# Row maxima taken one row-tile pair earlier, and a third PSUM buffer in the three feed-forward stages

## The chip, the cores and the metric

The kernel runs on all 8 cores of one Trainium2 chip, with no exchange between the cores. The metric is the time on the device in microseconds (us) of the slowest core; the figure shown for a kernel is the median of its runs.

## The reference, cut to what matters

The input x is 4 sequences of 4096 tokens with 1024 features, in float32. One layer is computed, attention first and then a gated feed-forward part, each behind a layer norm without weights:

```python
q = x @ Wq; k = x @ Wk; v = x @ Wv          # x is the normed input, 64 features out
att = softmax(einsum('bid,bkd->bik', q, k), axis=1)   # over i, the query axis
x = x + tile(att @ v, 16)
xr = mu_r*z + (1-mu_r)*z_prev;  xk = mu_k*z + (1-mu_k)*z_prev   # z = layernorm(x)
r = sigmoid(xr @ W_r.T);  k_act = relu(xk @ W_k.T)**2
x = x + r * (k_act @ W_v.T)
```

The softmax runs over the query axis, so a row-tile of 128 keys needs one maximum and one sum for each of its keys over all 4096 queries, and the sum is folded into the rows of v.

## The kernel before, in words

Two cores share a sequence. Each norms all 4096 tokens and computes attention for them, and then does the feed-forward part for its own 2048. The program is written engine by engine; its stages follow one another through counting semaphores (SM for TensorE, SV for VectorE, SS for ScalarE). The order on each engine is the order in which its instructions are written, and the counts waited for are computed by small functions (`d_max`, `d_ellsum`, `d_exp`, `d_outmm`, `i_sig`, `j_relu`, `k_tmp`), so a reordering of VectorE's work needs a new count for each of its instructions.

**Attention (lines 519 to 590, here stage D).** There are 32 row-tiles kt of 128 keys, worked in 16 groups q of two (a = 0 and 1, kt = 2q + a). A group has eight units: s = 0 to 3 (a stretch of 1024 queries), and in each of them a = 0, then a = 1. A unit is two score matmuls (L548, 64 rows, 512 columns each) into one of three PSUM units, then one exponential on ScalarE (L608) with the negated maximum as bias, which also leaves a partial sum in `ellp`. Below, the units of a group are u0 to u7. In program order:

- TensorE, group q: it first does the eight "out" matmuls (L529) of group q-2, which wait for the scaled v of that group, and then the 16 score matmuls of u0 to u7. A unit's scores wait for the exponential three units earlier, which frees its PSUM unit. Out matmuls and the next group's u0 therefore stand behind u7's scores of the group before.
- ScalarE, group q: eight exponentials. Before u0 and u1 (s = 0) it waits, in this order, for the row-tile's maximum (`d_max(kt)`), for the sum of the row-tile two earlier (`d_ellsum(kt-2)`, since that one's partial sums lie in the same columns of `ellp`), for out matmuls that free the buffer `p_sb` (`d_outmm(kt-4)`), and for the unit's scores (`d_smm`).
- VectorE, group q (lines 568 to 590): two maxima (L573, over every fourth column of the first 512 of u0 and of u1), then for each of the two row-tiles, once its eighth part's exponential is done, the sum (L579), its reciprocal (L583), the scaling of v (L586) and a small copy (L589).

In VectorE's order of before, the maxima of group q+1 stand behind all eight small instructions of group q.

**Feed-forward.** Stage H (L866 to L888) forms xr and xk: ScalarE scales, VectorE adds. Stage I (L899 to L923): 16 tiles of 16 matmuls (L909) into two PSUM buffers `rps` of 1024 columns, each evacuated by a sigmoid (L922); ScalarE waits for the end of stage H before its first sigmoid, while TensorE starts as soon as xr is complete. Stage J (L940 to L977): 32 tiles of 8 matmuls (L949) into two buffers `ktp` of 512 columns, relu on ScalarE (L965), square on VectorE (L974). Stage K (L997 to L1063): 16 tiles of 16 matmuls (L1006) into two buffers `ops` of 1024 columns; VectorE multiplies by r (L1051), adds attention's output (L1055) and x (L1061), and SyncE's queue writes y (L1029). In all three, TensorE waits for the reader of the tile two earlier before it reuses a buffer (L906, L947, L1003).

Of the kernel before, what the change touches and what calls it, by code (L numbers as in the profile page):

```python
# [7 lines left out]
F32 = mybir.dt.float32  # L8
BF16 = mybir.dt.bfloat16
AF = mybir.ActivationFunctionType  # L10
# [4 lines left out]
C = 1024  # L15
# [4 lines left out]
KT = 32  # L20
# [6 lines left out]
def build_program(debug=False):  # L27
    nc = bass.Bass("TRN2", target_bir_lowering=False)
# [32 lines left out]
    with ctx:  # L61
# [32 lines left out]
        def opens(cms):  # L94
            return [cm.__enter__() for cm in cms]
# [38 lines left out]
        SV = e(nc.semaphore("SV"))  # L134
        SS = e(nc.semaphore("SS"))
# [70 lines left out]
        SM_D0, SS_D0, SV_D0 = SM_C, SS_A, SV_C  # L206
# [12 lines left out]
                return SM_D0 + d_P(q + 2) - 4 * (1 - (t % 2))  # L219
            return SM_D0 + 368 + 8 * (q - 14) + 4 * (t % 2 + 1)  # L220
        d_exp = lambda kt, s: SS_D0 + 8 * (kt // 2) + 2 * s + (kt % 2) + 1
        d_max = lambda kt: SV_D0 + 10 * (kt // 2) + (kt % 2) + 1
        d_ellsum = lambda kt: SV_D0 + 10 * (kt // 2) + 3 + 4 * (kt % 2)
        d_recip = lambda kt: SV_D0 + 10 * (kt // 2) + 4 + 4 * (kt % 2)
        d_vsc = lambda kt: SV_D0 + 10 * (kt // 2) + 5 + 4 * (kt % 2)
        d_xp = lambda kt: SV_D0 + 10 * (kt // 2) + 6 + 4 * (kt % 2)
        SM_D = SM_D0 + 384
        SS_D = SS_D0 + 128
        SV_D = SV_D0 + 160
        e_evac = SV_D + 2  # L230
        e_tpmm = lambda b: SM_D + b + 1
        e_oxmm = SM_D + 16 + KT
# [58 lines left out]
        i_sig = lambda t: SS_I0 + t + 1  # L291
# [4 lines left out]
        j_relu = lambda ix: SS_J0 + ix + 1  # L296
# [6 lines left out]
        k_tmp = lambda t: SV_K0 + 3 * t + 1  # L303
# [261 lines left out]

        @block.vector
        def _(v):
            for q in range(KT // 2):
                for a in range(2):
                    kt = 2 * q + a  # L570
                    u0 = d_eidx(kt, 0) % 3
                    v.wait_ge(SM, d_smm(kt, 1))
                    v.reduce_max(negm[:, kt:kt + 1],  # L573
                                 units[u0][:, 0:512:4],
                                 axis=AX.X, negate=True).then_inc(SV, 1)
                for a in range(2):
                    kt = 2 * q + a
                    v.wait_ge(SS, d_exp(kt, 3))
                    v.reduce_sum(ell[:, kt:kt + 1],  # L579
                                 ellp[:, 4 * (kt % 2):4 * (kt % 2) + 4],  # L580
                                 axis=AX.X).then_inc(SV, 1)
                    v.wait_ge(SV, d_ellsum(kt))
                    v.reciprocal(rell[:, kt:kt + 1], ell[:, kt:kt + 1]).then_inc(SV, 1)  # L583
                    v.wait_ge(SV, d_recip(kt))
                    v.wait_ge(SVT, 16 * (kt + 2))
                    v.tensor_scalar(vs_sb[:, kt * D:(kt + 1) * D],  # L586
                                    v_sb[:, kt * D:(kt + 1) * D],
                                    rell[:, kt:kt + 1], None, ALU.mult).then_inc(SV, 1)
                    v.tensor_copy(xp_sb[:, kt:kt + 1],  # L589
                                  p_sb[kt % 4][:, 4095:4096]).then_inc(SV, 1)  # L590

        @block.scalar
        def _(sc):
# [299 lines left out]
        closes(z1T_cm)  # L893
        r_sb_cm = [nc.sbuf_tensor("r_sb", [128, TOWN * C], BF16, side="right")]
        r_sb, = opens(r_sb_cm)
        cm_rps = [nc.psum_tensor(f"rps{i}", [128, C], F32) for i in range(2)]
        r_ps = opens(cm_rps)

        @block.tensor  # L899
        def _(t):  # L900
            t.wait_ge(SV, h_xr_all)
            t.wait_ge(SS, SS_F)
            t.wait_ge(SWB, SWB_ALL)
            for t_ in range(TOWN):
                if t_ >= 2:
                    t.wait_ge(SS, i_sig(t_ - 2))  # L906
                for ct in range(CT):
                    for hh in range(2):
                        ins = t.matmul(  # L909
                            r_ps[t_ % 2][:, hh * 512:(hh + 1) * 512],  # L910
                            xr[ct][:, t_ * 128:(t_ + 1) * 128],
                            wrT[:, ct * C + hh * 512:ct * C + (hh + 1) * 512],
                            start=(ct == 0), stop=(ct == CT - 1),
                            skip_group_check=True)
                ins.then_inc(SM, 1)

        @block.scalar
        def _(sc):
            sc.wait_ge(SV, SV_H)
            for t_ in range(TOWN):  # L920
                sc.wait_ge(SM, i_mm(t_))
                sc.activation(r_sb[:, t_ * C:(t_ + 1) * C], r_ps[t_ % 2][:, :],  # L922
                              AF.Sigmoid).then_inc(SS, 1)  # L923

        closes(cm_rps)
# [8 lines left out]

        kaT_cm = [nc.sbuf_tensor(f"kaT{i}", [128, 2048], BF16, side="right") for i in range(CT)]
        kaT = opens(kaT_cm)
        cm_ktp = [nc.psum_tensor(f"ktp{i}", [128, 512], F32) for i in range(2)]
        kt_ps = opens(cm_ktp)

        @block.tensor  # L940
        def _(t):
            t.wait_ge(SS, SS_I)
            for dt in range(CT):
                for tc in range(4):
                    ix = dt * 4 + tc
                    if ix >= 2:
                        t.wait_ge(SS, j_relu(ix - 2))  # L947
                    for ct in range(CT):
                        ins = t.matmul(  # L949
                            kt_ps[ix % 2][:, :],  # L950
                            wkT[:, ct * C + dt * 128:ct * C + (dt + 1) * 128],
                            xk[ct][:, tc * 512:(tc + 1) * 512],
                            start=(ct == 0), stop=(ct == CT - 1),
                            skip_group_check=True)
                    ins.then_inc(SM, 1)

        @block.scalar
        def _(sc):
            for dt in range(CT):
                for tc in range(4):  # L960
                    ix = dt * 4 + tc
                    sc.wait_ge(SM, j_mm(ix))
                    if ix >= 4:
                        sc.wait_ge(SV, j_sq(ix - 4))
                    sc.activation(kaT[dt][:, tc * 512:(tc + 1) * 512],  # L965
                                  kt_ps[ix % 2][:, :], AF.Relu).then_inc(SS, 1)

        @block.vector
        def _(v):
# [21 lines left out]
        k32_cm = [nc.sbuf_tensor("tmp32", [128, 2 * C], F32, side="right"),  # L991
                  nc.sbuf_tensor("x2b", [128, 2 * C], F32, side="right")]
        tmp32, x2b = opens(k32_cm)
        cm_ops = [nc.psum_tensor(f"ops{i}", [128, C], F32) for i in range(2)]
        o_ps = opens(cm_ops)

        @block.tensor  # L997
        def _(t):
            t.wait_ge(SV, SV_J)
            t.wait_ge(SS, SS_J)  # L1000
            for t_ in range(TOWN):
                if t_ >= 2:
                    t.wait_ge(SV, k_tmp(t_ - 2))  # L1003
                for dt in range(CT):
                    for hh in range(2):
                        ins = t.matmul(  # L1006
                            o_ps[t_ % 2][:, hh * 512:(hh + 1) * 512],
                            kaT[dt][:, t_ * 128:(t_ + 1) * 128],
                            wvT[:, dt * C + hh * 512:dt * C + (hh + 1) * 512],
                            start=(dt == 0), stop=(dt == CT - 1),  # L1010
                            skip_group_check=True)
                ins.then_inc(SM, 1)
# [29 lines left out]
        @block.vector  # L1042
        def _(v):
            for t_ in range(TOWN):
                s = t_ % 4
                v.wait_ge(SM, k_mm(t_))
                v.wait_ge(SS, i_sig(t_))
                if t_ >= 2:
                    v.wait_ge(SV, k_x2(t_ - 2))
                    v.wait_ge(YSs[t_ % 2], ys_k(t_ - 2))  # L1050
                v.tensor_tensor(tmp32[:, (t_ % 2) * C:(t_ % 2 + 1) * C],  # L1051
                                o_ps[t_ % 2][:, :],
                                r_sb[:, t_ * C:(t_ + 1) * C], ALU.mult).then_inc(SV, 1)
                v.wait_ge(SV, k_tmp(t_))
                v.tensor_tensor(tmp32[:, (t_ % 2) * C:(t_ % 2 + 1) * C],  # L1055
                                tmp32[:, (t_ % 2) * C:(t_ % 2 + 1) * C],
                                bass.AP(out_tok, t_ * D, [[TOWN * D, 128], [0, 16], [1, D]]),
                                ALU.add).then_inc(SV, 1)
                v.wait_ge(FSs[t_ % 8], fs_k(t_))
                v.wait_ge(SV, k_mid(t_))  # L1060
                v.tensor_tensor(x2b[:, (t_ % 2) * C:(t_ % 2 + 1) * C],  # L1061
                                tmp32[:, (t_ % 2) * C:(t_ % 2 + 1) * C],
                                xst[:, (t_ % 8) * C:(t_ % 8 + 1) * C], ALU.add).then_inc(SV, 1)  # L1063
# [59 lines left out]
```

## Time and profile before

| what | value |
|---|---|
| median of 2 runs | 727.45 us (727.39 to 727.5) |
| the profiled execution | 728.75 us |
| its span, slowest core (core 3) | 727.1 us |
| spans of the eight cores | 717.6 to 727.1 us |
| mean granted TensorE clock of the cores | 0.706 to 0.729 of full speed |
| busy share: TensorE matmul, VectorE, ScalarE | 50%, 41%, 38% |

The span reaches from the first to the last instruction of one core; the run's time has 1.65 us more (728.75 less 727.1), which lie around it. A row of the profile gives a start, a duration, the engine, the line of the program, the output and input names, and in brackets how long the engine sat idle before and what released it. The granted clock is 1 at 2.4 GHz and 0.5 at 1.2 GHz. Times of single instructions on core 3 are given from the start of its span.

### The profile page before, as it was taken

The numbers are of one execution on the slowest core, as the hardware profiler recorded it, in microseconds if no ns is written. First come the engines' busy times: TensorE is split into PE (matmuls) and PEld (weight loads), VectorE is DVE, ScalarE is ACT, GpSimd is POOL, SyncE is SP. The second block draws the span as 40 slices with busy tenths as digits, with TensorE's granted clock in tenths as the row PEclk, the third lists the DMA queues.
The fourth block names the chain that finished last, engine by engine and source line by source line (L and its number), as shares of the span: only waits on it lengthen the run. The fifth ranks groups of instructions, "written<-read, shape, count | busy, mean of one in ns | idle before, by whom it ended". The sixth has DMA issues, their size and how long they took to land.

```text
span 727.1 us, 5705 instructions; the slowest of 8 cores (717.6 to 727.1 us)
## 1 busy us (share of the span) xinstructions
PE 362.9 (50%) x1392; PEld 124.3 (17%) x1392; DVE 296.7 (41%) x515; ACT 276.4 (38%) x437; POOL 25.4 (3%) x45
## 2 busy tenths in 40 slices
PE   0004000007967888888862000000439999999873
PEld 0001000003411111111112000000114434444331
DVE  3904508057711111111121598806860002228886
ACT  3205022050038898889860233206842233320000
POOL 2000000000000030000000011000000000011110
PEclk9999555557985555555565555555569999999997
DMA  9965977827010099900000044293100000007774
GB/s 235 284 160 132 276 115 250 191 80 173 1 32 7 6 138 160 288 7 0 1 0 1 5 165 181 71 178 73 29 0 1 0 1 1 0 21 269 255 227 154
DMA packets 79044, 75.82 MB, mean 104 GB/s; under 512 B 59427, under 2 KB 59443, under 8 KB 78948
## 3 DMA queue, kind: packets, MB, share of 16 engines
q1 hardware_dynamic: 25700, 41.01, 17.6%
q0 software_dynamic: 10944, 23.93, 14.2%
q10 hardware_dynamic: 42368, 10.52, 8.8%
q8 instruction: 12, 0.20, 0.1%
q14 instruction: 20, 0.16, 0.1%
HBM read 47.79 MB, written 21.56 MB: 95 GB/s over the span
## 4 chain that ended last, share of the span: by engine, by line
DMA 31%; PE 22%; DVE 20%; issue 12%; ACTq 7%; ACT 6%; SPq 2%; DVEq 1%
DMA v_sb<-vdram 14%; PE ktp L949 7%; PE rps L909 7%; ACTq L366 5%; DMA zdram<-zst 4%; DMA z1T<-z1dram 4%; DMA y_out<-x2b 4%; ACT p_sb L608 3%; DVE x1b L739 3%; DVE xk L888 3%; DVE sums L419 2%; DVE zst L407 2%; ACTq L831 2%; DMA xst<-x_in 2%; DVE tmp L1055 2%
## 5 line engine op out<-in xcount | busy, mean ns | idle before, releaser
L608 ACT ACTIVATE p_sb<-dpool,negm 128x1024 bf16<-128x1024 f32 x128 | 140.6, 1124 | 21.9 <-DVE negm L573 21.9
L909 PE MATMUL rps<-wrT,xr 128*128 128x512 bf16 x256 | 60.4, 402 | 142.0 <-DVE xr L881 130.0
L548 PE MATMUL dpool<-qrep,krep 64*128 64x512 bf16 x256 | 109.9, 601 | 33.6 <-ACT p_sb L608 28.3
L447 PE MATMUL qk<-zT,wqk 128*128 128x512 bf16 x64 | 18.1, 434 | 160.1 <-DVE qrep L478 98.5
L352 ACT ACTIVATE zst<-xst 128x1024 bf16<-128x1024 f32 x32 | 33.8, 1057 | 97.6 <-issue 86.0
L1006 PE MATMUL ops<-wvT,kaT 128*128 128x512 bf16 x256 | 57.2, 379 | 11.3 <-DVE tmp L1051 9.7
L579 DVE TENSOR_REDUCE ell<-ellp 128x1 f32<-128x4 f32 x32 | 5.0, 157 | 134.7 <-ACT p_sb L608 134.7
L949 PE MATMUL ktp<-xk,wkT 128*128 128x512 bf16 x256 | 55.6, 379 | 1.7 <-ACT r_sb L922 1.3
L909 PEld LDWEIGHTS rps<-wrT,xr 128*128 128x128 bf16 x256 | 26.2, 103 | 175.9 <-issue 148.9
L974 DVE TENSOR_TENSOR kaT<-kaT 128x512 bf16<-128x512 bf16 x32 | 13.6, 425 | 98.1 <-ACT kaT L965 98.0
L419 DVE TENSOR_REDUCE sums<-xst 128x1 f32<-128x1024 f32 x32 | 37.1, 1211 | 10.9 <-DMA xst<-x_in 10.9
L548 PEld LDWEIGHTS dpool<-qrep,krep 64*128 64x128 bf16 x256 | 16.7, 104 | 125.0 <-issue 124.8
L447 PEld LDWEIGHTS qk<-zT,wqk 128*128 128x128 bf16 x64 | 6.7, 107 | 169.5 <-issue 163.9
L376 DVE TENSOR_SCALAR smean<-sums,cconst 128x4 f32<-128x4 f32 x12 | 2.8, 229 | 78.4 <-ACT zst L352 76.9
L965 ACT ACTIVATE kaT<-ktp 128x512 bf16<-128x512 f32 x32 | 19.0, 597 | 34.5 <-PE ktp L949 34.5
L1006 PEld LDWEIGHTS ops<-wvT,kaT 128*128 128x128 bf16 x256 | 24.2, 97 | 44.3 <-issue 16.8
L816 ACT ACTIVATE zst<-x1b 128x1024 bf16<-128x1024 f32 x16 | 16.9, 1057 | 36.1 <-DVE x1b L739 36.1
L949 PEld LDWEIGHTS ktp<-xk,wkT 128*128 128x128 bf16 x256 | 24.9, 98 | 32.3 <-issue 2.6
L922 ACT ACTIVATE r_sb<-rps 128x1024 bf16<-128x1024 f32 x16 | 16.3, 1024 | 36.6 <-PE rps L909 36.6
L881 DVE SCALAR_TENSOR_TENSOR xr<-z1T,mu1m,xr 128x2048 bf16<-128x2048 bf16 x8 | 18.8, 2351 | 26.8 <-ACT xr L866 26.7
L608 ACT ACTIVATION_READ_ACCUMULATOR p_sb<-dpool,negm 128x1 f32 x128 | 27.7, 216 | 0.0
L529 PE MATMUL dpool<-p_sb,v_sb 128*64 128x512 bf16 x112 | 26.9, 634 | 0.0
(83 smaller groups left out, 371.8 us busy)
## 6 DMA issues: line engine op xcount, KB each, us to landing
xst<-x_in SPq DMA_DIRECT2D x32, 512.0 KB, 9.0
xst<-x_in POOLq DMA_DIRECT2D x32, 512.0 KB, 7.2
zdram<-zst SPq DMA_DIRECT2D x32, 256.0 KB, 7.7
y_out<-x2b SPq DMA_DIRECT2D x16, 512.0 KB, 4.2
z1dram<-z1b SPq DMA_DIRECT2D x16, 256.0 KB, 3.2
wrT<-wrT_in POOLq DMA_DIRECT2D x1, 2048.0 KB, 18.8
wkT<-wkT_in POOLq DMA_DIRECT2D x1, 2048.0 KB, 30.7
wvT<-wvT_in POOLq DMA_DIRECT2D x1, 2048.0 KB, 44.0
```

The source lines that it names most:

```text
L352: sc.activation(zst[:, (i % 8) * C:(i % 8 + 1) * C], xst[:, (i % 8) * C:(i % 8 + 1) * C], AF.Square, accum_out=sumsq[:, i % 8:i % 8 + 1]). ...
L366: sc.dma_start(out=zT[ctn][:, qtr * 1024:(qtr + 1) * 1024], in_=zdram[qtr * 1024:(qtr + 1) * 1024, ctn * 128:(ctn + 1) * 128], transpose=T ...
L419: v.reduce_sum(sums[:, i % 8:i % 8 + 1], xst[:, (i % 8) * C:(i % 8 + 1) * C], axis=AX.X).then_inc(SV, 1)
L447: t.matmul(qk[buf][:, :], wqk[:, ct * 128:(ct + 1) * 128], zT[ct][:, nch * 512:(nch + 1) * 512], start=(ct == 0), stop=(ct == CT - 1), ski ...
L529: t.matmul(dpool[64 * half:64 * half + 64, (w % 2) * 512:(w % 2) * 512 + 512], vs_sb[:, tt_ * D:(tt_ + 1) * D], p_sb[tt_ % 4][:, w * 512:( ...
L548: t.matmul(units[u][:, cc * 512:(cc + 1) * 512], krep[64 * a:64 * (a + 1), kt * 128:(kt + 1) * 128], qrep[64 * a:64 * (a + 1), c * 512:(c ...
L608: sc.activation(p_sb[kt % 4][:, s * 1024:(s + 1) * 1024], units[u][:, :], AF.Exp, bias=negm[:, kt:kt + 1], accum_out=ellp[:, 4 * (kt % 2) + s:
L739: v.tensor_tensor(x1b[:, s8 * C:(s8 + 1) * C], xst[:, s8 * C:(s8 + 1) * C], bass.AP(out_tok, t_ * D, [[TOWN * D, 128], [0, 16], [1, D]]), ...
L888: v.scalar_tensor_tensor(xk[ct][:, :], z1T[ct][:, 15:2063], mu1m[:, 8 + ct:9 + ct], xk[ct][:, :], ALU.mult, ALU.add).then_inc(SV, 1)
L909: ins = t.matmul(r_ps[t_ % 2][:, hh * 512:(hh + 1) * 512], xr[ct][:, t_ * 128:(t_ + 1) * 128], wrT[:, ct * C + hh * 512:ct * C + (hh + 1) ...
L949: ins = t.matmul(kt_ps[ix % 2][:, :], wkT[:, ct * C + dt * 128:ct * C + (dt + 1) * 128], xk[ct][:, tc * 512:(tc + 1) * 512], start=(ct == ...
L1006: ins = t.matmul(o_ps[t_ % 2][:, hh * 512:(hh + 1) * 512], kaT[dt][:, t_ * 128:(t_ + 1) * 128], wvT[:, dt * C + hh * 512:dt * C + (hh + 1) ...
```

## The change

It does two things. In attention, VectorE takes the maxima of groups 0 and 1 first, and then, behind the eight small instructions of group q, the maxima of group q+2 instead of q+1; the counts are recomputed by a table. In stages I, J and K the PSUM buffers are three instead of two, and TensorE waits for the reader of the tile three earlier.

```diff
+        D_CNT = {}
+        _sv = SV_D0
+        for _kt in range(4):
+            _sv += 1
+            D_CNT[("max", _kt)] = _sv
+        for _q in range(16):
+            for _a in range(2):
+                _kt = 2 * _q + _a
+                for _op in ("ellsum", "recip", "vsc", "xp"):
+                    _sv += 1
+                    D_CNT[(_op, _kt)] = _sv
+            if _q + 2 < 16:
+                for _a in range(2):
+                    _sv += 1
+                    D_CNT[("max", 2 * (_q + 2) + _a)] = _sv
+        d_max = lambda kt: D_CNT[("max", kt)]
...
         @block.vector
         def _(v):
-            for q in range(KT // 2):
+            def d_maxes(v, q):
                 for a in range(2):
                     kt = 2 * q + a
                     u0 = d_eidx(kt, 0) % 3
...
                     v.reduce_max(negm[:, kt:kt + 1],
                                  units[u0][:, 0:512:4],
                                  axis=AX.X, negate=True).then_inc(SV, 1)
+
+            d_maxes(v, 0)
+            d_maxes(v, 1)
+            for q in range(KT // 2):
                 for a in range(2):
                     kt = 2 * q + a
                     v.wait_ge(SS, d_exp(kt, 3))
...
+                if q + 2 < KT // 2:
+                    d_maxes(v, q + 2)
...
-        cm_rps = [nc.psum_tensor(f"rps{i}", [128, C], F32) for i in range(2)]
+        cm_rps = [nc.psum_tensor(f"rps{i}", [128, C], F32) for i in range(3)]
...
-                if t_ >= 2:
-                    t.wait_ge(SS, i_sig(t_ - 2))
+                if t_ >= 3:
+                    t.wait_ge(SS, i_sig(t_ - 3))
...
-        cm_ktp = [nc.psum_tensor(f"ktp{i}", [128, 512], F32) for i in range(2)]
+        cm_ktp = [nc.psum_tensor(f"ktp{i}", [128, 512], F32) for i in range(3)]
...
-                    if ix >= 2:
-                        t.wait_ge(SS, j_relu(ix - 2))
+                    if ix >= 3:
+                        t.wait_ge(SS, j_relu(ix - 3))
...
-        cm_ops = [nc.psum_tensor(f"ops{i}", [128, C], F32) for i in range(2)]
+        cm_ops = [nc.psum_tensor(f"ops{i}", [128, C], F32) for i in range(3)]
...
-                if t_ >= 2:
-                    t.wait_ge(SV, k_tmp(t_ - 2))
+                if t_ >= 3:
+                    t.wait_ge(SV, k_tmp(t_ - 3))
```

The indices of the buffers change from `% 2` to `% 3` with it, in the matmuls and in their readers.

## Rows read from the trace of the kernel before

**Rows 1.** Page, costliest groups: the exponentials, with the idle time before them.

```profile
L608 ACT ACTIVATE p_sb<-dpool,negm 128x1024 bf16<-128x1024 f32 x128 | 140.6, 1124 | 21.9 <-DVE negm L573 21.9
```

**Rows 2.** Timeline of TensorE alone, core 3: one group's out matmuls in attention.

```profile
260.77 1.92 PE L529 MATMUL dpool<-p_sb,v_sb 128*64 128x512 bf16 x8
```

**Rows 3.** The same, matmuls that run between 262.9 and 263.2 us.

```profile
262.62 1.04 PE L548 MATMUL dpool<-qrep,krep 64*128 64x512 bf16 x4
```

**Rows 4.** Timeline of all engines, core 3, the same group change.

```profile
254.10 1.11 ACT L608 ACTIVATE p_sb<-dpool,negm 128x1024 bf16<-128x1024 f32 x1 [1.47 <-DVE negm L573]
...
259.47 0.22 ACT L608 ACTIVATION_READ_ACCUMULATOR p_sb<-dpool,negm 128x1 f32 x1
...
259.80 0.14 PEld L548 LDWEIGHTS dpool<-qrep,krep 64*128 64x128 bf16 x2 [0.96 <-issue]
...
261.99 0.16 DVE L579 TENSOR_REDUCE ell<-ellp 128x1 f32<-128x4 f32 x1 [7.95 <-ACT p_sb L608]
262.25 0.16 DVE L583 RECIPROCAL rell<-ell 128x1 f32<-128x1 f32 x1
...
262.74 0.24 ACT L608 ACTIVATION_READ_ACCUMULATOR p_sb<-dpool,negm 128x1 f32 x1
...
263.08 0.16 DVE L579 TENSOR_REDUCE ell<-ellp 128x1 f32<-128x4 f32 x1 [0.20 <-ACT p_sb L608]
...
263.84 0.15 DVE L589 COPY xp_sb<-p_sb 128x1 bf16<-128x1 bf16 x1
263.90 0.48 DVE L573 TENSOR_REDUCE negm<-dpool 128x1 f32<-128x128 f32 x2
264.44 1.11 ACT L608 ACTIVATE p_sb<-dpool,negm 128x1024 bf16<-128x1024 f32 x1 [1.47 <-DVE negm L573]
```

**Rows 5.** Line 573's durations in ns (least, median, most), core 3.

```profile
L573 DVE TENSOR_REDUCE negm<-dpool x32: 277/280/292, 207.8 to 367.5; 128x1 f32<-128x128 f32 x32
```

**Rows 6.** Timelines of single engines, core 3, start of attention and its first group change.

```profile
207.13 0.61 PE L548 MATMUL dpool<-qrep,krep 64*128 64x512 bf16 x4 [0.94 <-DVE p_sb L482]
...
207.82 0.49 DVE L573 TENSOR_REDUCE negm<-dpool 128x1 f32<-128x128 f32 x2 [0.84 <-PE dpool L548]
...
222.59 0.48 DVE L573 TENSOR_REDUCE negm<-dpool 128x1 f32<-128x128 f32 x2
...
220.33 0.23 ACT L608 ACTIVATION_READ_ACCUMULATOR p_sb<-dpool,negm 128x1 f32 x1
...
223.07 1.11 ACT L608 ACTIVATE p_sb<-dpool,negm 128x1024 bf16<-128x1024 f32 x1 [1.41 <-DVE negm L573]
```

**Rows 7.** Stretches: TensorE busy (matmuls), clock, DMA share, GB/s; core 0, then core 3.

```profile
214.00:368.00 154.00, 118.36 (x354) 0.63 0.37 72
...
214.00:368.00 154.00, 129.73 (x352) 0.50 0.37 72
```

**Rows 8.** Timeline, core 3, start of the sigmoid stage.

```profile
519.50 9.83 PE L909 MATMUL rps<-wrT,xr 128*128 128x512 bf16 x32 [130.00 <-DVE xr L881]
...
541.38 18.86 PE L909 MATMUL rps<-wrT,xr 128*128 128x512 bf16 x77 [12.04 <-ACT r_sb L922]
545.60 14.36 PEld L909 LDWEIGHTS rps<-wrT,xr 128*128 128x128 bf16 x67 [0.28 <-issue]
```

**Rows 9.** Timeline, core 3, start of the relu stage.

```profile
593.23 3.61 PE L949 MATMUL ktp<-xk,wkT 128*128 128x512 bf16 x16 [1.26 <-ACT r_sb L922]
...
597.23 2.97 PE L949 MATMUL ktp<-xk,wkT 128*128 128x512 bf16 x13 [0.39 <-ACT kaT L965]
```

**Rows 10.** Line 1051, core 3: what it waited for, then who waited for it.

```profile
  DMA y_out<-x2b: 7.9, 6
  PE ops L1006: 4.0, 1
...
  PE ops L1006: 9.7, 11
```

More of the change, by code:

```diff
@@ L221, in build_program @@
         d_exp = lambda kt, s: SS_D0 + 8 * (kt // 2) + 2 * s + (kt % 2) + 1
[L222 to L226, printed above, removed]
+        D_CNT = {}
[14 more added lines that the diff above has]
+        d_max = lambda kt: D_CNT[("max", kt)]
+        d_ellsum = lambda kt: D_CNT[("ellsum", kt)]
+        d_recip = lambda kt: D_CNT[("recip", kt)]
+        d_vsc = lambda kt: D_CNT[("vsc", kt)]
+        d_xp = lambda kt: D_CNT[("xp", kt)]
         SM_D = SM_D0 + 384
         SS_D = SS_D0 + 128
-        SV_D = SV_D0 + 160
+        SV_D = _sv
+        assert SV_D == SV_D0 + 160
         e_evac = SV_D + 2
@@ L909, in _ @@
                         ins = t.matmul(
-                            r_ps[t_ % 2][:, hh * 512:(hh + 1) * 512],
+                            r_ps[t_ % 3][:, hh * 512:(hh + 1) * 512],
                             xr[ct][:, t_ * 128:(t_ + 1) * 128],
@@ L921, in _ @@
                 sc.wait_ge(SM, i_mm(t_))
-                sc.activation(r_sb[:, t_ * C:(t_ + 1) * C], r_ps[t_ % 2][:, :],
+                sc.activation(r_sb[:, t_ * C:(t_ + 1) * C], r_ps[t_ % 3][:, :],
                               AF.Sigmoid).then_inc(SS, 1)
@@ L945, in _ @@
                     ix = dt * 4 + tc
-                    if ix >= 2:
-                        t.wait_ge(SS, j_relu(ix - 2))
+                    if ix >= 3:
+                        t.wait_ge(SS, j_relu(ix - 3))
                     for ct in range(CT):
                         ins = t.matmul(
-                            kt_ps[ix % 2][:, :],
+                            kt_ps[ix % 3][:, :],
                             wkT[:, ct * C + dt * 128:ct * C + (dt + 1) * 128],
@@ L965, in _ @@
                     sc.activation(kaT[dt][:, tc * 512:(tc + 1) * 512],
-                                  kt_ps[ix % 2][:, :], AF.Relu).then_inc(SS, 1)
+                                  kt_ps[ix % 3][:, :], AF.Relu).then_inc(SS, 1)
         @block.vector
@@ L1006, in _ @@
                         ins = t.matmul(
-                            o_ps[t_ % 2][:, hh * 512:(hh + 1) * 512],
+                            o_ps[t_ % 3][:, hh * 512:(hh + 1) * 512],
                             kaT[dt][:, t_ * 128:(t_ + 1) * 128],
@@ L1051, in _ @@
                 v.tensor_tensor(tmp32[:, (t_ % 2) * C:(t_ % 2 + 1) * C],
-                                o_ps[t_ % 2][:, :],
+                                o_ps[t_ % 3][:, :],
                                 r_sb[:, t_ * C:(t_ + 1) * C], ALU.mult).then_inc(SV, 1)
```

## The prediction

> **What bounds the kernel now.** I read the page's costliest groups first. The exponentials of attention are its largest item, 140.6 us, with 21.9 us of idle time before them, all put down to the maxima [rows 1]: 15 group changes at 1.46 us. This is what the new order of VectorE addresses. The question is what holds the exponential once the maximum no longer stands behind eight other instructions, so next I took the timelines around one group change, TensorE alone [rows 2, 3] and all engines [rows 4].
>
> ScalarE's period is 10.34 us (254.10 to 264.44): eight exponentials at 1.09, and a wait of 1.47. The last exponential's accumulator read ends at 262.98, yet u0 of the next group starts at 264.44 [rows 4]. VectorE is busy with its small instructions until 263.99 and starts the maxima at 263.90. TensorE, though, is hardly earlier. u7's scores could only be written once u4's exponential had ended at 259.69; they start by 259.83, the eight out matmuls follow at 260.77, and the next group's u0 scores not before 262.62 [rows 2 to 4]. Four score matmuls, those of u0 and u1, overlap and end at 262.62 + 1.04 = 263.66 [rows 3]. So two chains, through VectorE and through TensorE, end within 0.24 us of each other (263.66 and 263.90), and only the first is shortened.
>
> For the feed-forward stages I read the gaps of TensorE. Stage I starts with two tiles at 519.50, ends them at 529.33, and then waits 12.04 us for the first sigmoid, which ScalarE cannot start before stage H is done [rows 8]. After that TensorE runs without a gap. Stage J has a gap of 0.39 us before its third tile [rows 9]. In stage K TensorE waits 9.7 us for VectorE, while VectorE waits only once for TensorE, at the start (4.0 us), and 7.9 us for writes of y [rows 10].
>
> **Attention, steady group changes (14 of the 15).** The maxima's release moves from VectorE's own queue to TensorE's semaphore. At the start of the stage four matmuls end at 207.13 + 0.61 = 207.74, and the maximum that they release starts at 207.82 [rows 6]: 0.08 us. So maximum 0 starts at 263.66 + 0.08 = 263.74 instead of 263.90. Two maxima take 0.48 and one of them 0.28, so the second starts 0.20 behind the first [rows 4, 5], at 263.94, and ends at 264.22.
>
> That would give back 0.16, but there is a second edge. ScalarE's u0 also waits for the sum of the row-tile two earlier, L579. Before, that sum was done at 262.15, long ahead. In the new order it is queued behind both maxima of the next group, which wait for TensorE. It starts when they have passed: an instruction without a dependency starts about 0.09 before the end of the one ahead (copy to 263.99, maximum at 263.90) [rows 4], so at 264.13, and ends 0.16 later at 264.29. Then ScalarE: before, maximum 0 ended at 264.18 and the exponential began at 264.44, 0.26 later, with three more waits in its queue. At the first group change, where there are two more, it is 222.59 + 0.28 to 223.07, 0.20 [rows 5, 6]. I read 0.06 for each further wait. Behind the sum two are left, so 0.20: the exponential starts at 264.49, 0.05 later than before. Times 14, +0.7 us.
>
> Its bounds: if the sum did not count, 263.74 + 0.28 + 0.26 = 264.28, a gain of 0.16 each or 2.2 us in all. If u1's matmuls came a slot of 0.43 later than I read (4 matmuls in 1.04 us against 604 to 635 ns for one leaves little room), nothing on VectorE overlapped, and each step paid the 0.10 between a sum and its reciprocal (262.15 to 262.25), the start would be 263.66 + 0.43 + 0.08 + 0.28 + 0.10 + 0.16 + 0.20 = 264.91, a loss of 0.47 each or 6.6 us. I stay with +0.05, since the pairing is seen in rows 3. Behind the waiting maxima stand also reciprocal, scaling and copy of both row-tiles. The scaled v is needed by out matmuls a whole group later, and the second sum must be there for u1, 1.09 us behind u0. From a sum to the start of what follows its copy is 0.82 (263.08 to 263.90) [rows 4], so the second sum runs from 264.95 to 265.11 and would let u1 go at 265.31, against 264.49 + 1.09 = 265.58: hidden, with 0.27 of cover. If that cover were gone, u1 would take over as the one that waits.
>
> **The first group change** has no out matmuls in TensorE's queue. There u6's exponential ends at 220.56 [rows 6], u1's scores start 0.25 later and take a slot and a matmul (0.43 + 0.61), to 221.85; maximum at 221.93 to 222.21, sum to 222.28, exponential with one further wait (0.14) at 222.42 instead of 223.07: -0.65, between 0 and -1.4 (the whole wait). Attention together: +0.7 - 0.65, about +0.1 us, from -3.6 to +6.6.
>
> **Stage I.** With a third buffer, tile 2 is computed inside the 12.04 us wait. It costs 16 slots; in the fast stretch 67 weight loads take 14.36 us, 0.215 each [rows 8], so 3.45 us. It fits, leaving 8.6 idle, and 13 tiles instead of 14 stand behind the first sigmoid: -3.45 us. The clock: the first stretch after the wait runs at half speed, from 541.38 to 545.60, about 10 slots of 0.43. I keep that cost, since 8.6 us of idle are left. If it vanished, another 10 x 0.21 = 2.1 us would go; if it were as much longer, 2.1 come back.
>
> **Stage J.** The 0.39 us before the third tile [rows 9] go, as its buffer is free: -0.39, between 0 and that. Nothing else waits there. **Stage K.** TensorE's 9.7 us of waits are off the chain: VectorE has three instructions of 1.23 to a tile, and waits for writes of y. TensorE runs one tile further ahead, and nobody starts sooner. 0 us.
>
> The Trainium skill (Perfetto Trace Analysis, Optimization Strategy) says that a gap that keeps repeating on the engine that should be saturated can mean that too few buffers fit in SBUF or PSUM. Stage K's waits on TensorE have that look, and by that rule the third buffer would give them back; here the rows of VectorE say that TensorE is not that engine. It is a rival below.
>
> **Sum.** 728.75 + 0.1 - 3.45 - 0.39 = 725.0 us for the profiled execution. That one ran 1.30 above the median of 727.45, so 723.7 us for the median.
>
> **Rivals.**
> - *The wait of ScalarE closes.* For it: all 21.9 us are put down to the maxima [rows 1]. Against it: TensorE's u0 at 262.62. Then the time is 723.7 - 0.1 - 21.9 = 701.7. TensorE at full clock would do most of it: u7's, the out and u0's matmuls take eight slots or so at half speed. With slots of 0.21, u1's scores would follow u6's exponential (ended 261.88) as at the first group change but quicker, at 262.7, and the exponential could start at 263.25, -1.19 each, 17 us in all, so about 706. On core 3 the clock stood at 0.50 over the 154 us; on core 0 it was 0.63 on average [rows 7], and since a core's place in the order by time can change, some chance stays. Chance of either 0.06. The Trainium skill (TensorE: Matmul & The Clock Gate, on why this matters for kernels) holds that TensorE kept busy without gaps gets the full clock; core 3, busy for 9 of 10.3 us, shows that this doesn't come by itself.
> - *Stage K gives back TensorE's 9.7 us.* For it: 11 waits for L1051; against it: VectorE's only wait for TensorE is the first tile's. 723.7 - 9.7 = 714.0. Chance 0.05.
> - *The sum behind the maxima costs more (slower).* One place: L579 behind L573 in VectorE's queue, with ScalarE's u0 behind it. At its upper bound attention loses 6.6 - 0.65, and the total is 728.75 + 5.95 - 3.84 = 730.9, or 729.6 against the median. The change turns slower than before once a group change costs over 0.32 us more (14 x 0.32 = 4.5, as much as the other terms give). For it: three serial steps behind a late TensorE; against: the overlaps seen in rows 3 and 4. Chance 0.12.
> - *The new order gains nothing and the rest neither* (the idle stretch in stage I costs more cold slots, or writes of y in stage K eat what comes early, as their 7.9 us depend on what else moves): 726 to 729. Chance 0.10.
>
> **How the numbers follow.** My forecast, 723.7 with its own 719.5 to 726, has 0.67. The range of 8 in 10 is 719.5 to 728.5: it has the forecast's low end (attention -2.2 and the cold stretch gone -2.1, near 719.5) and most of the last two rivals; about 0.11 lies below, in the two fast rivals, and under 0.09 above. A measurement of this kernel tells about 2%, 14.5 us, from no change. Faster by over that, under 712.9, is only the first rival: 0.06. Slower by over that, above 742, has no case that I can price: 0.02. Within 2%: 0.92.
>
> **What would show it.** In the changed profile: the wait before u0's exponential still about 1.5 us at 14 of 15 group changes, now put down to the sum L579 (or TensorE) rather than L573; the maxima starting 0.08 us behind TensorE's matmuls and ahead of L579; a first group change about 0.8 us wide; stage I starting with 48 matmuls in a row and about 8.6 us of idle behind them; no wait of 0.39 in stage J; in stage K fewer waits of TensorE and the same length from first L1051 to the end. A group change under 1 us wide would overturn the reading of TensorE's chain; a shorter stage K, that of VectorE's.

## The result, and the profile after

The changed kernel runs in 723.8 us (median of 21 runs, 721.1 to 730.7) against 730.1 us for the kernel before in the same rounds (median of 20, 726.3 to 733.5). The ratio is 0.9923, with a 95% interval of 0.9902 to 0.9944: a gain of 0.8%. The forecast was 723.7 against 727.45, a ratio of 0.9948, with the range 719.5 to 728.5. The kernel before has medians of 727 to 734 us in the different sets of runs, so ratios are used from here on; they leave out the few executions in which the cores ran longer at a lower granted clock.

The profiled execution took 725.28 us, with a span of 723.7 on its slowest core, now core 1. Its costliest groups, next to [rows 1]:

```profile
L630 ACT ACTIVATE p_sb<-dpool,negm 128x1024 bf16<-128x1024 f32 x128 | 140.5, 1124 | 22.3 <-PE dpool L564 17.0
L931 PE MATMUL rps<-wrT,xr 128*128 128x512 bf16 x256 | 59.6, 398 | 141.7 <-DVE xr L903 132.6
...
L589 DVE TENSOR_REDUCE negm<-dpool 128x1 f32<-128x128 f32 x32 | 7.9, 287 | 129.9 <-PE dpool L564 129.9
L1028 PE MATMUL ops<-wvT,kaT 128*128 128x512 bf16 x256 | 56.5, 379 | 6.7 <-DVE tmp L1073 5.2
```

The exponentials' idle time is 22.3 us where it was 21.9, and has changed its name: most of it is now put down to TensorE's scores instead of the maxima, and the maxima themselves wait for TensorE, 129.9 us in all. The program's lines have moved: 573 is now 589, 608 is 630, 548 is 564.

A group change of attention, timeline of all engines on core 1 (start, duration, engine, line, what; in brackets the idle time before), next to [rows 3, 4]:

```profile
257.47 1.92 PE L545 MATMUL dpool<-p_sb,v_sb 128*64 128x512 bf16 x8
...
259.32 1.89 PE L564 MATMUL dpool<-qrep,krep 64*128 64x512 bf16 x6
259.43 0.24 ACT L630 ACTIVATION_READ_ACCUMULATOR p_sb<-dpool,negm 128x1 f32 x1
...
260.46 0.49 DVE L589 TENSOR_REDUCE negm<-dpool 128x1 f32<-128x128 f32 x2 [7.99 <-PE dpool L564]
260.87 0.15 DVE L599 TENSOR_REDUCE ell<-ellp 128x1 f32<-128x4 f32 x1
261.12 0.16 DVE L603 RECIPROCAL rell<-ell 128x1 f32<-128x1 f32 x1
261.22 1.11 ACT L630 ACTIVATE p_sb<-dpool,negm 128x1024 bf16<-128x1024 f32 x1 [1.55 <-PE dpool L564]
...
271.64 1.11 ACT L630 ACTIVATE p_sb<-dpool,negm 128x1024 bf16<-128x1024 f32 x1 [1.55 <-PE dpool L564]
```

The order is the one that the prediction drew: eight out matmuls, u0's and u1's scores at 259.32, both maxima at 260.46, the sum behind them at 260.87, and the exponential at 261.22. The period is 10.42 us (261.22 to 271.64) where it was 10.34. The profile names TensorE as the releaser; the sum ended at 261.02, later than anything of TensorE's that this exponential needs, so the name alone would mislead.

The start of the sigmoid stage and of the relu stage, timeline of core 1, next to [rows 8, 9]:

```profile
519.98 12.88 PE L931 MATMUL rps<-wrT,xr 128*128 128x512 bf16 x48 [132.65 <-DVE xr L903]
...
541.85 3.55 PE L931 MATMUL rps<-wrT,xr 128*128 128x512 bf16 x8 [9.00 <-ACT r_sb L944]
...
589.84 12.46 PE L971 MATMUL ktp<-xk,wkT 128*128 128x512 bf16 x57 [1.26 <-ACT r_sb L944]
```

48 matmuls now run before the wait instead of 32, the wait is 9.00 instead of 12.04 us, and in stage J the matmuls run on past the second tile. Line 1073 (L1051 before), what it waited for and then who waited for it, next to [rows 10]:

```profile
  DMA y_out<-x2b: 8.5, 5
  PE ops L1028: 4.0, 1
...
  PE ops L1028: 5.2, 7
```

TensorE waits less in stage K: 5.2 us on this core, where the same core had 6.7 before and core 3 had 9.7. VectorE waits as before. By stage, from the first and last start of the stages' lines on each core, the means of the eight cores:

| stage (us) | before | after | forecast for the difference |
|---|---|---|---|
| attention, first to last exponential | 162.65 | 162.4 | +0.1 |
| I, first matmul to stage J's first | 73.5 | 70.4 | -3.45 |
| J, to stage K's first matmul | 57.5 | 57.0 | -0.39 |
| K, first matmul to the last L1061 (L1083) | 70.6 | 70.7 | 0 |

The mean of attention hides two kinds of cores: 162.8 to 163.1 us on six, 161.0 and 160.6 on cores 3 and 4. The start of attention and the stretch from its end to stage I differ by some us from core to core and from run to run in both kernels.

### The profile page after: what moved, and what is told of

Same layout as the page of the kernel before. It is cut to its first block, busy times and chain, and to the rows that moved or that the text cites. A ratio compares the mean times of both kernels' runs of the same rounds, so it can differ in the third digit from the quotient of the medians.

```text
span 723.7 us, 5702 instructions; the slowest of 8 cores (712.3 to 723.7 us)
## 1 busy us (share of the span) xinstructions
PE 356.0 (49%) x1392; PEld 124.5 (17%) x1392; DVE 295.6 (41%) x515; ACT 276.2 (38%) x437; POOL 25.4 (4%) x45
## 4 chain that ended last, share of the span: by engine, by line
DMA 30%; PE 28%; DVE 19%; issue 9%; ACTq 7%; ACT 5%; SPq 2%; DVEq 1%
DMA v_sb<-vdram 13%; PE ktp L971 8%; PE rps L931 6%; ACTq L382 5%; DMA zdram<-zst 4%; DMA z1T<-z1dram 4%; PE dpool L564 4%; DMA xst<-x_in 3%; DMA y_out<-x2b 3%; PE ops L1028 3%; DVE x1b L761 3%; DVE xk L910 3%; ACT p_sb L630 2%; DVE sums L435 2%; ACTq L853 2%
## 5 line engine op out<-in xcount | busy, mean ns | idle before, releaser
L630 ACT ACTIVATE p_sb<-dpool,negm 128x1024 bf16<-128x1024 f32 x128 | 140.5, 1124 | 22.3 <-PE dpool L564 17.0
L564 PE MATMUL dpool<-qrep,krep 64*128 64x512 bf16 x256 | 104.0, 575 | 39.8 <-DVE xp_sb L609 19.8
L589 DVE TENSOR_REDUCE negm<-dpool 128x1 f32<-128x128 f32 x32 | 7.9, 287 | 129.9 <-PE dpool L564 129.9
```

What stands on the lines that cost most here:

```text
L564: t.matmul(units[u][:, cc * 512:(cc + 1) * 512], krep[64 * a:64 * (a + 1), kt * 128:(kt + 1) * 128], qrep[64 * a:64 * (a + 1), c * 512:(c ...
L630: sc.activation(p_sb[kt % 4][:, s * 1024:(s + 1) * 1024], units[u][:, :], AF.Exp, bias=negm[:, kt:kt + 1], accum_out=ellp[:, 4 * (kt % 2) + s:
```

## The experiments

Nine runs follow: eight kernels, one of them twice. Each is set against the kernel before as it ran in the same rounds.

### e1_order: VectorE's order alone

```diff
 (the change, with the buffers of stages I, J and K back at two)
-        cm_rps = [nc.psum_tensor(f"rps{i}", [128, C], F32) for i in range(3)]
+        cm_rps = [nc.psum_tensor(f"rps{i}", [128, C], F32) for i in range(2)]
...
```

> Only VectorE's new order; stages I, J, K keep two buffers. Theory (TensorE's chain through u7's scores, the eight out matmuls and u0's scores sets the exponential of u0 as much as VectorE did, and the sum L579 is now queued behind the waiting maxima): attention keeps its length, a group change costs 10.42 us instead of 10.34 (10.24 on a core whose clock rises inside u0's scores), the first change 0.67 instead of 1.41. Time within 1 us of before, ratio 0.997 to 1.002. Rival (the order of VectorE was what held ScalarE, and the gain of the change is its): 3 to 6 us faster, ratio 0.992 to 0.996.

Measured: 729.25 against 728.56 us, ratio 1.0005 (0.997 to 1.004). Attention: 162.8 and 162.9 us on cores 2 and 5, 160.6 to 161.1 on the other six. The first and last exponential of core 5, what it waited for, and then the same of core 0:

```profile
L630 ACT ACTIVATE p_sb<-dpool,negm x128: 1106/1122/1152, 212.4 to 375.3; 128x1024 bf16<-128x1024 f32 x128
...
  PE dpool L564: 17.0, 11
  DVE ell L599: 5.0, 4
```

```profile
L630 ACT ACTIVATE p_sb<-dpool,negm x128: 1103/1120/1147, 207.5 to 368.1; 128x1024 bf16<-128x1024 f32 x128
...
  DVE ell L599: 19.8, 15
```

The wait of 22 us is there on core 5, and 19.8 us of it on core 0: the new order removed the cause that was named [rows 1], and the wait stayed. The 2 us that six cores save in attention don't show in the time (ratio 1.0005). The rival, that the gain of the change is the order's, falls.

### e2_buffers: the third buffers alone

```diff
 (the kernel before, with)
-        cm_rps = [nc.psum_tensor(f"rps{i}", [128, C], F32) for i in range(2)]
+        cm_rps = [nc.psum_tensor(f"rps{i}", [128, C], F32) for i in range(3)]
...
 (ktp and ops and the three waits likewise)
```

> Only the third buffers in stages I, J and K; VectorE's old order. Theory: stage I shorter by 3.2 us, J by 0.5, K unchanged, so -3.7 us, ratio 0.995, nearly all that the change brings. Rival (order of VectorE brings it): under 1 us. Rival (stage K gives back its waits too): K shorter by several us and the ratio under 0.985.

Measured: 726.26 against 728.56 us, ratio 0.9948 (0.9915 to 0.998). Stage I is 70.2 to 71.0 us on the eight cores, J 56.9 to 57.0, attention 162.6 to 162.9. This is the change's gain, within the intervals. The product of the two parts' ratios, 1.0005 x 0.9948 = 0.9953, lies just above the change's interval (0.9902 to 0.9944), and well within what the parts' own intervals allow.

### e7_k_only: the third buffer in stage K alone

```diff
 (the kernel before, with)
-        cm_ops = [nc.psum_tensor(f"ops{i}", [128, C], F32) for i in range(2)]
+        cm_ops = [nc.psum_tensor(f"ops{i}", [128, C], F32) for i in range(3)]
...
-                if t_ >= 2:
-                    t.wait_ge(SV, k_tmp(t_ - 2))
+                if t_ >= 3:
+                    t.wait_ge(SV, k_tmp(t_ - 3))
```

> The third buffer in stage K alone. Theory: stage K keeps its length of 70.6 us on average over the cores, since VectorE waits for writes of y and not for TensorE, ratio 0.997 to 1.003. Rival (the 9.7 us in which TensorE waited come back): ratio near 0.987, stage K near 61 us.

Measured: ratio 0.9994 (0.9961 to 1.0028). Stage K takes 66.9 to 71.9 us on the eight cores, 69.8 on average; in e1, with two buffers, it takes 69.1. L1051 on core 7, waits and waiters:

```profile
  DMA y_out<-x2b: 6.8, 3
  PE ops L1006: 4.0, 1
...
  PE ops L1006: 4.2, 3
```

TensorE's waits fell to 4.2 us on this core, where it had 7.4 before (means of the eight cores: 3.6 and 7.3), and nothing came of it. The rule of the Trainium skill that the prediction named (Perfetto Trace Analysis, Optimization Strategy) speaks of the engine that should be saturated; here that is VectorE, with three instructions of 1.23 us to a tile, and its waits are for writes of y.

### e3_sums: the sum's edge taken away

```diff
 (the change, with)
-                                 ellp[:, 4 * (kt % 2):4 * (kt % 2) + 4],
+                                 ellp[:, 4 * (kt % 4):4 * (kt % 4) + 4],
...
-                            if kt >= 2:
-                                sc.wait_ge(SV, d_ellsum(kt - 2))
+                            if kt >= 4:
+                                sc.wait_ge(SV, d_xp(kt - 4))
...
 (accum_out of the exponential likewise into column 4 * (kt % 4) + s)
```

> The change, and each of four row-tiles in flight gets its own four columns of partial sums, so that ScalarE's u0 waits for the copy of the row-tile four earlier and no longer for the sum that is queued behind the maxima. Theory: u0's exponential starts 1.68 us behind u0's scores instead of 1.90, a group change of 10.2 us; about 3 us less than the change if the sum is the last edge. Rival (TensorE alone sets it and the sum was hidden): no difference, group change 10.42.

Measured: ratio 0.9895 (0.9858 to 0.9932), where the change alone has 0.9923. Attention takes 159.1 to 159.6 us on the eight cores. Its exponentials at two successive group changes, timeline of ScalarE, core 0:

```profile
309.91 1.11 ACT L630 ACTIVATE p_sb<-dpool,negm 128x1024 bf16<-128x1024 f32 x1 [1.34 <-DVE ell L599]
320.12 1.11 ACT L630 ACTIVATE p_sb<-dpool,negm 128x1024 bf16<-128x1024 f32 x1 [1.34 <-DVE ell L599]
```

The wait is 1.34 instead of 1.55, the period 10.21 instead of 10.42: beside the cores of the change at 10.42, the sum cost 0.21 us at each change, as its place in the chain said (0.22). Within the chain it is the same: from u0's scores (308.21) to the exponential are 1.70 us instead of 1.90. With the first group change, whose 0.67 us of wait are gone, that makes 14 x 0.21 + 0.67 = 3.6 us, which is 163.0 less 159.4. Beside the cores at 10.24 (see below) it is 0.03 a change. The rest of the wait is TensorE's, as e4 shows. (The releaser printed is the sum again, for which this kernel doesn't wait there: it ended last before the exponential began.)

### e4_spread_sums: TensorE's queue cleared as well

```diff
 (e3, with)
-                if q >= 2:
-                    for tt_ in (2 * (q - 2), 2 * (q - 2) + 1):
-                        (wait, and the four out matmuls of tt_)
...
                             t.matmul(units[u][:, cc * 512:(cc + 1) * 512],
...
+                        if q >= 1 and 2 * s + a == 3:
+                            d_outs(2 * (q - 1))
+                        if q >= 1 and 2 * s + a == 5:
+                            d_outs(2 * (q - 1) + 1)
...
 (d_smm and d_outmm from a table of TensorE's new order; the last two row-tiles' out matmuls at the end)
```

> As e3, and TensorE does the out matmuls of group q-1 inside group q, four behind u3's scores and four behind u5's, instead of all eight ahead of group q+1. Theory (TensorE's queue ahead of u0's scores holds the exponential): ScalarE's wait at a group change falls from 1.5 us to 0.1 or less, 15 times, so some 19 to 21 us off attention and a time near 704. Rival (TensorE at half clock has no room for the out matmuls anywhere, since 8 units of 0.86 and 4 slots of 0.43 make 8.6 us of 8.74): waits appear inside the group instead and the gain is under half, 6 to 10 us. Rival (the wait at a group change is VectorE's): none.

Measured: 704.11 against 728.56 us, ratio 0.9648 (0.9595 to 0.9701). Attention takes 141.1 to 141.4 us on the eight cores. The exponentials on core 0: first and last start, and who waited for whom.

```profile
L644 ACT ACTIVATE p_sb<-dpool,negm x128: 1104/1120/1169, 212.9 to 354.0; 128x1024 bf16<-128x1024 f32 x128
...
  DMA vdram<-p_sb: 49.0, 1
```

The only wait left in front of an exponential is the one at the start of the stage. 162.65 less 141.3 are 21.4 us, nearly the 21.9 us of [rows 1], and it took three edits: the maxima's place on VectorE, the out matmuls on TensorE, and the sum for which ScalarE waits. The 127 steps from the first exponential to the last would be 138.4 us at 1.09 each; the other 2.9 us lie inside the groups, where one step in each is 1.27 (269.40 to 270.67 on core 0), the one to u4, whose scores stand behind four out matmuls.

### e5_spread_old and e6_spread: each without one of the others

```diff
 (e5: the kernel before with third buffers and e4's order of TensorE; VectorE's order and ellp as before)
 (e6: the change with e4's order of TensorE; ellp as before)
```

> Third buffers, VectorE's old order (the maxima of a group behind all small instructions of the group before), and TensorE's out matmuls spread as in e4. Theory (two chains end close together, each alone holds the exponential): freeing TensorE alone gives nothing, attention stays at 162.6 to 162.8 us from first to last exponential, time as e2_buffers, ratio about 0.995. Rival (TensorE's queue was the only bound and VectorE's order plays no part): attention near 141 us and about 704 to 706.

Measured: ratio 0.9964 (0.9929 to 1.0); attention 165.0 to 165.3 us. On core 5:

```profile
L622 ACT ACTIVATE p_sb<-dpool,negm x128: 1103/1113/1142, 216.9 to 381.9; 128x1024 bf16<-128x1024 f32 x128
...
  DVE negm L587: 21.9, 15
```

The 21.9 us stand unchanged, under the maxima's name. That attention grew by 2.4 us was not expected: the period is 10.48 instead of 10.34 (timeline: exponentials of u0 at 279.81 and 290.29), with the wait at the group change as before, so 0.14 us went inside the group, where e4 has its loss too: u4's exponential follows u3's after 1.24 us (283.09 to 284.33) instead of 1.09.

> The change with TensorE's out matmuls spread as in e4, but the partial sums shared as before, so that u0 waits for the sum L579 behind both maxima. Theory (the sum's edge costs what it did at the first group change of the changed kernel, where TensorE had no out matmuls: 0.67 us idle, some 0.8 us of period): attention near 141.3 + 15 x 0.8 = 153 us, time near 716. Rival (the sum costs only its 0.22 us, as in steady state of the change): attention near 145, time near 708. Rival (no cost): as e4.

Measured: 720.9 against 733.55 us, ratio 0.9837 (0.9792 to 0.9882); attention 151.0 to 151.5 us. Two of its group changes (timeline of ScalarE, core 6):

```profile
286.02 1.11 ACT L644 ACTIVATE p_sb<-dpool,negm 128x1024 bf16<-128x1024 f32 x1 [0.31 <-DVE ell L613]
295.76 1.11 ACT L644 ACTIVATE p_sb<-dpool,negm 128x1024 bf16<-128x1024 f32 x1 [0.73 <-PE dpool L575]
```

With TensorE out of the way, the shared columns of partial sums cost 151.4 - 141.3 = 10.1 us, three times what they cost behind TensorE (0.21 x 14 = 3). Both waits are the sum's, whatever the name: in front of the exponential of 295.76 it ended at 295.56, 0.20 us earlier. So under TensorE's chain lay a third one, through the sum, and cutting the first two alone gives back only half.

### e9_pairs, and e4 again

```diff
 (e4, with the out matmuls of group q-1 two at a time, w = 0 and 2 and then 1 and 3)
-        behind the scores of u3 (four) and u5 (four)
+        behind the scores of u2, u3 (row-tile 0) and u5, u6 (row-tile 1), two each
```

> As e4, but the out matmuls of group q-1 come in pairs (two halves of the array, one slot of 0.43 us) behind u2's, u3's, u5's and u6's scores of group q, instead of four behind u3's and four behind u5's. Theory (in e4 four out matmuls at a time hold up u4's scores, so u4's exponential comes 1.27 us behind u3's instead of 1.09, 15 times 0.18): attention shorter by some 2.5 us than e4's 141.3, near 139, and the time 2 us below e4 in the same call. Rival (the slots are only pushed to another unit, as 8.6 us of TensorE in 8.74 leave no room): attention 141 or longer.

> The kernel of e4 once more, on this chip, to set e9 against and to see whether its gain over before holds: ratio 0.96 to 0.97, attention 141.3 us.

Measured: e4 again 699.85 against 727.13 us, ratio 0.9617 (0.9573 to 0.9661), attention 141.1 to 141.3. e9 703.08, ratio 0.9674 (0.9622 to 0.9726), attention 145.8 to 145.9: 4.5 us longer, where 2.5 shorter was expected. This is a miss. Timeline of TensorE alone in e9, core 7:

```profile
269.60 1.04 PE L575 MATMUL dpool<-qrep,krep 64*128 64x512 bf16 x4
270.57 0.64 PE L554 MATMUL dpool<-p_sb,v_sb 128*64 128x512 bf16 x2
271.14 1.03 PE L575 MATMUL dpool<-qrep,krep 64*128 64x512 bf16 x2
272.11 0.64 PE L554 MATMUL dpool<-p_sb,v_sb 128*64 128x512 bf16 x2
272.68 3.70 PE L575 MATMUL dpool<-qrep,krep 64*128 64x512 bf16 x8
276.68 0.64 PE L554 MATMUL dpool<-p_sb,v_sb 128*64 128x512 bf16 x2 [0.31 <-DVE ell L613]
...
278.78 1.04 PE L575 MATMUL dpool<-qrep,krep 64*128 64x512 bf16 x4
```

The starts are what to look at. A pair of out matmuls, one slot of 0.43 us (the time from one pair's start to the next at half clock), holds the next scores back by 0.57 (270.57 to 271.14), and two score matmuls of one unit hold the outs back by 0.97 (271.14 to 272.11) for 0.86. So a change between the two kinds costs 0.11 to 0.14 us each time. e4 changes four times in a group, e9 eight times, which is 4 x 0.12, half a microsecond more.

That is not all that e9 changed. Its first pair of out matmuls stands one unit earlier than e4's, behind u2's scores, and TensorE sits idle 0.31 us in front of it in each group, 15 times and 5.0 us in all; in e4 again (core 4) TensorE never waits in front of an out matmul. The pair needs the scaled v, which VectorE has ready only at 276.43 (timeline of all engines, same core):

```profile
276.19 0.24 DVE L620 TENSOR_SCALAR v_sb<-v_sb,rell 128x64 bf16<-128x64 bf16 x1 [0.17 <-DVE rell L617]
```

The period is 9.18 us (269.60 to 278.78), of which TensorE is busy 8.87; in e4 it is 8.90 (270.67 to 279.57 on core 0). As an estimate from these rows, 9.18 - 0.31 and 9.18 - 0.48 are both below 8.90: without the wait e9 would not be longer than e4, and without the added changes it would not be either, so both seem to have a part in the 4.5 us. No run separates them. In 230 to 340 us (columns: length of the stretch, then busy time and count of TensorE, its weight loads, VectorE, ScalarE and GpSimd; granted clock; DMA):

```profile
230.00:340.00 110.00, 103.80 (x288) 17.64 (x288) 19.53 (x118) 106.09 (x193) 6.88 (x11) 0.50 0.51 100
```

TensorE has little room left there, and ScalarE now waits for it in every group. In e4 again (core 4) ScalarE is busy for 109.64 of the same 110 us, and TensorE for 95.39 at a mean clock of 0.60:

```profile
230.00:340.00 110.00, 95.39 (x297) 17.40 (x296) 20.99 (x129) 109.64 (x199) 6.89 (x11) 0.60 0.51 100
```

The version to keep is e4: 3.5 and 3.8% faster than the kernel before in its two runs.

## Why the prediction was right

**The reading of two chains held.** The prediction said that through TensorE u0's exponential could not come earlier than through VectorE. e1 shows it (ratio 1.0005), and with e4, e5 and e6 every step is there, in us of attention: VectorE freed alone gives nothing on the cores at 10.42 and 2 on those at 10.24 (e1), TensorE freed alone nothing (e5, 2.4 longer), both 11 (e6), and both with the sum 21 (e4).

**The steady group change: +0.05 forecast, +0.08 measured** on the cores whose clock stands at half in this chain. Step by step from u0's scores: maximum 1.14 us behind (forecast 1.12), sum 0.41 behind the maximum (0.39), exponential 0.35 behind the sum (0.36). The release of VectorE by TensorE took 0.10 and not 0.08. Nothing else in the chain was off by more than 0.02. u1 followed at 1.11, so the second sum was hidden, as said. Two readings in the prediction are loose, and nothing rests on them: eight exponentials at 1.09 and a wait of 1.47 make 10.19 and not 10.34, since the last exponential and its accumulator read take 1.25; and core 3's TensorE was busy for 8.7 and not 9 of 10.3 us (129.73 of 154 us) [rows 7].

**The first group change** was 0.67 us of idle instead of 1.41, -0.74, for -0.65.

**What the prediction did not have** is a second period. On cores 3 and 4 of the profiled run it is 10.24 and not 10.42, which is 2 us less in attention, and in e1 six cores of eight are like that. TensorE's granted clock rises there while u0's and u1's scores are running. Stretches on core 4, then on core 1, during these scores: TensorE busy (matmuls), granted clock, DMA:

```profile
307.00:307.25 0.25, 0.25 (x4) 0.67 0.19 45
307.25:307.50 0.25, 0.25 (x3) 1.00 0.06 1
...
260.00:260.25 0.25, 0.25 (x3) 0.50 0.76 131
260.25:260.50 0.25, 0.25 (x3) 0.50 1.04 197
```

It is not the rise as such that counts. Core 1 has one in each group as well from 292.50 on, but there it comes when u0's exponential has just begun (292.48), behind the chain, and the period stays 10.42. The prediction took the clock as 0.50 all through the chain; for the kernel before that made no difference, since VectorE stood in front: attention is 162.6 to 162.7 us on all its cores, with mean clocks from 0.50 to 0.64 in 230 to 340 us. The shorter period lies within the bound that was given for a group change (a gain of at most 0.16), and below the value taken.

**Stage I: -3.45 forecast, -3.1 measured.** A tile at full clock was computed in the wait, as said; the idle that was left is 9.00 us for 8.6. The missing 0.35 is in the clock term, which the prediction kept unchanged. Added up from the granted clock in the 12 us behind the wait, TensorE ran at half speed for 3.4 to 5.0 us on the eight cores before (mean 4.0) and for 3.4 to 5.6 after (mean 4.7). Half of the 0.65 us more is lost, 0.33. e1 and e2 agree: 4.5 and 4.9 us at half speed, stages of 73.8 and 70.5 us, and 3.25 + 0.2 is again 3.45. Why the stretch is longer was not shown. **Stage J: -0.39 forecast, -0.5 measured. Stage K: 0 and 0**, and e7 confirms it alone.

**The size of the whole** came out a little larger than forecast, 0.9923 against 0.9948, with the interval's upper end at 0.9944. That the median itself, 723.8, met the forecast of 723.7 is luck: the kernel before ran 2.7 us longer in these rounds than in the two runs that the forecast started from. The stage table accounts for 3.75 us of some 5.6. The shorter period on some cores can add up to 2 us where the slowest core has it; that it does so was not shown, and e1, where six cores have it, gained nothing. The rest may be the spread of the stages ahead of attention.

Of the rivals, the wait of ScalarE did not close with this change. Its price, 701.7 us or a ratio of 0.9646, is what e4 then reached with the other two edges cut (0.9648 and 0.9617). The other way to that price, TensorE at full clock, did not come: in 230 to 340 us the mean granted clock lay between 0.50 and 0.67 on every core of every profile, and in e9, where TensorE was busy for 103.80 of 110 us, it was 0.50 on all eight. The Trainium skill (TensorE: Matmul & The Clock Gate, on why this matters for kernels) would have TensorE at full clock when kept busy without gaps; e9 still has its gap of 0.31 us in each group, so no run here tests that.

## What to carry to other kernels

An idle time with one releaser in the profile is a wait for the last of what may be several chains. Before one is shortened, the end of each of the others is to be put beside it in one period of the timeline: here 263.66 stood against 263.90, and of the 21.9 us the maxima's new place gave back nothing alone, 0.13 us per change with the sum's wait gone as well (10.34 to 10.21, e3), and all but a little once TensorE's chain was cut too (e4). When an instruction that waits is moved forward on an in-order engine, whatever stands behind it is delayed to its release; here that was a sum for which the same consumer waited. A third buffer pays where the producer has an idle stretch to fill (stage I, 3 us), and nothing where the consumer is the bound (stage K).

## What the runs showed of the hardware that was not expected

- Changing between two kinds of matmuls on different parts of the array (64 rows by 128 columns, and 128 rows by 64 columns) cost 0.11 to 0.14 us of TensorE each time at half clock (e9, from the starts between 270.57 and 272.11). What part this has in e9's 4.5 us is open.
- The granted clock rose once per group on some cores and hardly at all on others running the same program (mean 0.67 on core 3, 0.54 on core 5 of the changed kernel, in 230 to 340 us). The period of the loop stayed at 10.24 us where the rise fell into u0's and u1's scores (cores 3 and 4), and was 10.42 us where it came behind them or not at all (cores 1 and 5).
- ScalarE started an exponential later after its last release the more satisfied waits still stood in its queue: 0.15 us with one (first group change of the changed kernel), 0.20 with two (both kernels), 0.26 with three (the kernel before). I read some 0.06 us for each.
